# A decoder layer on one core: attention scores in 32-row tiles opened and closed in two halves, k spread by GpSimd alone, and linear attention's turns, h and statistics at other places

## The reference

```python
# block 1
x = x + linear_attention(layernorm(x, ln1))  # 16 heads of 8; phi = elu + 1
#   kv = einsum('bshd,bshe->bhde', phi_k, v); z = sum_s phi_k
#   out = (phi_q kv) / (phi_q z + 1e-6) @ wo
x = x + lookup_gelu(layernorm(x, ln2) @ w1) @ w2   # input rounded to steps of 0.1
# block 2: cross attention with ctx, causal, rows of the queries masked
q, k, v = x @ WQ, ctx @ WK, ctx @ WV               # 16 heads of 8
scores = where(mask | future, -1e9, q k / sqrt(8)); out = softmax(scores) v @ WO
# block 3: a mixture of experts
out = x @ W_shared.T + (sum of the two gate weights) * (x @ W_expert.T) + bias
```

## Time and profile before

| | us |
|---|---|
| median of 3 runs | 599.19 (598.56 to 599.45) |
| the profiled execution | 602.87 |
| its span | 601.2 |
| TensorE busy | 527.9 (88%) |
| VectorE busy | 416.3 (69%) |
| ScalarE busy | 369.0 (61%) |
| GpSimd busy | 330.8 (55%) |

### The profile page before, as it was taken

One profiled execution on the slowest core, in us unless ns is written; L12 is line 12 of the kernel. 1 busy time (PEld: TensorE's weight loads), 2 busy tenths in 40 slices (PEclk: granted clock), 3 DMA queues, 4 the chain that ended last, 5 costly groups with the idle time before them and its releaser, 6 DMA issues.

```text
span 601.2 us, 22996 instructions
## 1 busy us (share of the span) xinstructions
PE 527.9 (88%) x9312; PEld 370.4 (62%) x9312; DVE 416.3 (69%) x1453; ACT 369.0 (61%) x643; POOL 330.8 (55%) x603
## 2 busy tenths in 40 slices
PE   2699998989999999988999999998989989999741
PEld 1467776656677767755666666666646656666530
DVE  2567777766767765375587778777867787779743
ACT  2356566557777777766766666666656666666520
POOL 6766667745755556341337554655465447554563
PEclk9899999999999999999999999999999999999876
DMA  5610000000000001001112111111111011111001
GB/s 160 188 38 3 3 1 2 3 3 1 1 2 1 2 5 26 1 11 28 27 32 49 29 40 33 49 30 43 29 48 28 27 48 50 28 34 22 20 19 35
DMA packets 24986, 17.97 MB, mean 30 GB/s; under 512 B 3120, under 2 KB 21424, under 8 KB 24880
## 3 DMA queue, kind: packets, MB, share of 16 engines
q1 hardware_dynamic: 24448, 16.43, 10.4%
q10 hardware_dynamic: 432, 0.07, 0.1%
HBM read 9.67 MB, written 4.19 MB: 23 GB/s over the span
## 4 chain that ended last, share of the span: by engine, by line
PE 58%; SPq 9%; ACT 8%; DVE 7%; issue 7%; POOL 6%; DMA 4%; POOLq 0%; DVEq 0%; ACTq 0%
SPq L394 8%; PE pair L1145 7%; PE pair L1179 7%; PE pair L1194 6%; PE pair L1213 6%; PE pair L1258 5%; PE pair L1114 5%; PE pair L1223 4%; PE pair L1036 4%; DMA k_exp<-k_sb 3%; ACT gel L718 3%; PE pair L1107 3%; PE pair L1232 2%; PE pair L1201 2%; PE pair L1049 2%
## 5 line engine op out<-in xcount | busy, mean ns | idle before, releaser
L718 ACT ACTIVATE gel<-pair 128x1024 f32<-128x1024 f32 x64 | 65.5, 1024 | 75.4 <-PE pair L1213 75.4
L926 DVE TENSOR_REDUCE neg_max<-pair 128x16 f32<-128x1024 f32 x64 | 60.9, 951 | 20.3 <-PE pair L1201 20.2
L1194 PE MATMUL pair<-k_exp,qT 64*32 64x256 f32 (+1 forms) x1024 | 57.5, 501 | 8.5 <-DMA k_exp<-k_sb 7.7
L1179 PEld LDWEIGHTS pair<-w,gel 128*128 128x128 f32 x512 | 60.3, 192 | 7.4 <-issue 5.5
L1223 PEld LDWEIGHTS pair<-v,gel 128*32 128x32 f32 x4096 | 41.7, 110 | 37.1 <-ACT gel L718 31.2
L1179 PE MATMUL pair<-w,gel 128*128 128x128 f32 x512 | 62.2, 276 | 1.0 <-ACT gel L643 1.0
L1223 PE MATMUL pair<-v,gel 128*32 128x18 f32 x4096 | 48.2, 187 | 15.5 <-ACT gel L718 12.8
L1145 PE MATMUL pair<-hT,w 128*128 128x512 f32 x128 | 58.5, 597 | 1.9 <-ACT lev L638 1.3
L712 ACT ACTIVATE gel<-gel,row_scale 128x512 f32<-128x512 f32 x80 | 54.4, 719 | 4.8 <-DVE gel L939 4.8
L303 POOL TENSOR_SCALAR veps_c<-mv_c 128x4 f32<-128x4 f32 x16 | 3.7, 229 | 96.0 <-issue 89.8
L303 POOL TENSOR_SCALAR veps_b<-mv_b 128x4 f32<-128x4 f32 x32 | 7.8, 245 | 81.6 <-DVE mv_b L295 45.8
(11 more groups left out here) (127 smaller groups left out, 1228.5 us busy)
## 6 DMA issues: line engine op xcount, KB each, us to landing
X<-in_x SPq DMA_DIRECT2D x16, 256.0 KB, 3.0
cT<-in_ctx SPq DMA_DIRECT2D x16, 256.0 KB, 2.9
out_rows<-X SPq DMA_DIRECT2D x16, 256.0 KB, 2.5
k_exp<-k_sb SPq DMA_DIRECT2D x160, 16.0 KB
w<-in_L_attn_w SPq DMA_DIRECT2D x2, 256.0 KB, 3.3
w_kv<-in_L_attn_wk SPq DMA_DIRECT2D x1, 64.0 KB, 3.2
w_q<-in_L_attn_wq ACTq DMA_DIRECT2D x1, 64.0 KB, 3.0
w_kv<-in_L_attn_wv SPq DMA_DIRECT2D x1, 64.0 KB, 3.1
```

What stands on the lines that cost most here:

```text
L718: nc.scalar.activation(pT[par], pair[par][:, :, :].rearrange("p a c -> p (a c)"), ACT.Copy).then_inc(pT_ready, 1)
L926: nc.vector.tensor_reduce(neg_max[par][:, :].rearrange("p (a h) -> p a h", a=2), scores, AX.X, ALU.max, negate=True).then_inc(max_ready, 1)
L1179: last = nc.tensor.matmul(bank(6 + q)[:, P * t:P * (t + 1)], gel[:, q, f, P * t:P * (t + 1)], w_2[:, f, :], start=(f == 0), stop=(f == NF ...
L1194: nc.tensor.matmul(pair[t % 2][b * QW:(b + 1) * QW, half, 0:HH * width], qT[p][rows, batch + first:batch + first + QW], keys, start=True, ...
```

## The change

- `k_exp` has 4 copies (HQ) instead of 8: in copy h only head h of each 32 rows is not zero. GpSimd makes all four with `quad_mask`; the DMAs, `kexp_loaded`, `zeroed` and the memsets are gone.
- A tile's scores are 16 matmuls on 32 rows each, of half the columns. `scores_open(n)` does the mask first, then quads 0 and 2; `scores_close(n)` waits for the opening (`s_opened`) and does quads 1 and 3. The two quads of a half write different columns of the same bank. Tile n + 2 is opened ahead of `weigh_values(n)`; tile n + 1 is closed at the head of slot t.
- Phase 1: TensorE turns the rows of s + 2 ahead of the k and v projection; ScalarE makes h ahead of the exponentials of k and the copy of v; VectorE attends ahead of phi_q and takes the statistics one group earlier, at the stage's end.
- GpSimd's constants go in five parts behind its stages 3 to 7 of phase 2, VectorE's behind stage 11. The first probabilities and the rows of ln_a change places on ScalarE.

```diff
@@ SyncE, phase3
-                if exists(s + 1):
-                    spread_k(s + 1, 1 - p)
@@ GpSimd
+            def late_constants(part):
+                if part == 0:
+                    const(nc.gpsimd.memset(quad_mask[:, :], 1.0))
+                    for b in range(4):
+                        m = quad_mask[b * QW:(b + 1) * QW, :]
+                        const(select(out=m, in_=m, compare_op=ALU.is_ge, fill=0.0, base=0,
+                                     pattern=[[-DH, HQ]], channel_multiplier=1))
...
+                if part == 1:
+                    const(nc.gpsimd.memset(causal[:, :, :], 0.0))
...
-                for h in range(HDMA, HH):
+                for h in range(HQ):
                     last = nc.gpsimd.tensor_scalar(k_exp[q][:, h, :], k_sb[:, :],
-                                                   half_mask[:, h:h + 1], 0.0, ALU.mult, ALU.add)
+                                                   quad_mask[:, h:h + 1], 0.0, ALU.mult, ALU.add)
...
-            for s in range(2):
-                zero(k_exp[s])
-
-            pipeline(pool, phase2, first=2, last=NG - 4)
+
+            for s in range(2, NG - 3):
+                phase2(s, s % 2)
+                if 3 <= s <= 7:
+                    pool.wait_ge(ln_a.offs, 2 * s)
+                    late_constants(s - 3)
@@ ScalarE, phase1: rows_h and rows_h2 ahead of the exponential of k and the copy of v
@@ ScalarE, head of phase 3
+            probabilities(0)
             rows_a(NG - 3, 1)
-            probabilities(0)
+            act.wait_ge(down_done, NG)
+            phase3(0, 0, slots=(0, 1))
             rows_a(NG - 2, 0)
-            act.wait_ge(down_done, NG)
-            phase3(0, 0, slots=(0,))
+            phase3(0, 0, slots=(2,))
             rows_a(NG - 1, 1)
-            phase3(0, 0, slots=range(1, TG))
+            phase3(0, 0, slots=(3,))
@@ VectorE, phase1
-                if exists(s + 3):
-                    statistics1(s + 3, 1 - p)
-                if second_norm(s + 3):
-                    statistics2(s + 3 - NG, 1 - p)
+                if s < 0:
+                    statistics1(2, 0)
+                if exists(s):
+                    attend(s, p)
...
-                if exists(s):
-                    attend(s, p)
...
+                if exists(s + 4):
+                    statistics1(s + 4, p)
+                if second_norm(s + 4):
+                    statistics2(s + 4 - NG, p)
@@ TensorE, phase1: xpose_rows and xpose_rows2(0) ahead of the k and v projection
@@ TensorE, phase2, stage NG - 1
-                    first_scores(0, 0)
+                    scores_open(0)
                 for t in range(TG):
+                    if t == 1 and s == NG - 1:
+                        scores_close(0)
@@ TensorE, phase3
+            def quad_scores(n, quads):
+                t, p = n % TG, n // TG % 2
                 first, width = (0, QW) if n % 2 else (QW, S)
+                for quad in quads:
+                    rows = slice(quad * QW, (quad + 1) * QW)
+                    heads = slice(quad % 2 * HQ * width, (quad % 2 + 1) * HQ * width)
                     for b in range(QB):
                         batch = (t // 2 * QB + b) * S
+                        last = nc.tensor.matmul(
+                            pair[t % 2][b * QW:(b + 1) * QW, quad // 2, heads],
+                            qT[p][rows, batch + first:batch + first + QW],
+                            k_exp[p][rows, :, batch:batch + width],
+                            start=False, stop=quad % 2 == 1)
+                return last
+
+            def scores_open(n):
+
+                after(pe, pT_ready, n - 1)
+                if n % TG == 0:
+                    pe.wait_ge(kexp_ready, n // TG + 1)
+                    pe.wait_ge(q_ready, n // TG + 1)
+                width = QW if n % 2 else S
                 for half in range(2):
                     rows = slice(half * FH, half * FH + QW)
                     future = causal_bf[rows, :].rearrange("p (h k) -> p h k", k=S)[:, :, S - width:]
                     for b in range(QB):
+                        nc.tensor.matmul(pair[n % 2][b * QW:(b + 1) * QW, half, 0:HH * width],
+                                         ident_bf[rows, rows], future, start=True, stop=False)
+                quad_scores(n, (0, 2)).then_inc(s_opened, 1)
+
+            def scores_close(n):
+
+                pe.wait_ge(s_opened, n + 1)
+                quad_scores(n, (1, 3)).then_inc(s_done, 1)
...
                 for t in slots:
-                    if t < TG - 1 and exists(s):
-                        scores(s * TG + t + 1, t + 1, p)
+                    if s == 0 and t == 0:
+                        scores_open(1)
+                    elif exists(s) and s * TG + t + 1 < NT:
+                        scores_close(s * TG + t + 1)
...
-                    if t == TG - 1 and exists(g):
-                        first_scores(g, q)
...
+                        if s * TG + t + 2 < NT:
+                            scores_open(s * TG + t + 2)
                         weigh_values(s * TG + t, t, p)
```

More of the change, by code:

```diff
@@ L153, in decoder_layer @@
             arena = early_memory.enter_context(nc.sbuf_tensor("arena", [P, ARENA], F32))
-        k_exp = [sb(f"k_exp{i}", [P, HH, GW]) for i in range(2)]
+        k_exp = [sb(f"k_exp{i}", [P, HQ, GW]) for i in range(2)]
         used = 0
@@ L223, in decoder_layer @@
             ("s_done", "max_ready", "sub_ready", "exp_ready"))
+        s_opened = sem("s_opened")
         p_xposed, pT_ready, pv_done = sem("p_xposed"), sem("pT_ready"), sem("pv_done")
@@ L454, in _ @@
                 rows1(i, i)
[L455 to L473, removed]
             def phase1(s, p):
@@ L615, in phase1 @@
                                          scale=-1.0).then_inc(expq_ready, 1)
+                if exists(s + 2):
+                    rows_h(s + 2, p)
+                if second_norm(s + 2):
+                    if s + 2 == NG:
+                        act.wait_ge(w_loaded, ALL_WEIGHTS)
+                    rows_h2(s + 2 - NG, p)
+                if exists(g):
                     act.wait_ge(kv_done, g + 1)
@@ L1018, in _ @@
             pipeline(dve, phase1, last=NG - 1)
-            pipeline(dve, phase2, first=0, last=NG // 2 - 1)
+            pipeline(dve, phase2, first=0, last=NG - 5)
             constants()
-            pipeline(dve, phase2, first=NG // 2, last=NG - 1)
+            pipeline(dve, phase2, first=NG - 4, last=NG - 1)
             phase3(-1, 1, slots=(2, 3))
@@ L1110, in phase1 @@
                     numerators(s, p)
+                if exists(s + 2):
+                    xpose_rows(s + 2, p)
+                if s + 2 == NG:
+                    xpose_rows2(0, p)
                 if exists(g):
@@ L1183, in phase2 @@
                     last.then_inc(down_done, 1)
-            def scores(n, t, p):
-                after(pe, pT_ready, n - 1)
+            def quad_scores(n, quads):
+                t, p = n % TG, n // TG % 2
                 first, width = (0, QW) if n % 2 else (QW, S)
-                for half in range(2):
-                    rows = slice(half * FH, (half + 1) * FH)
+                for quad in quads:
+                    rows = slice(quad * QW, (quad + 1) * QW)
+                    heads = slice(quad % 2 * HQ * width, (quad % 2 + 1) * HQ * width)
                     for b in range(QB):
                         batch = (t // 2 * QB + b) * S
-                        keys = k_exp[p][rows, :, batch:batch + width]
-                        nc.tensor.matmul(pair[t % 2][b * QW:(b + 1) * QW, half, 0:HH * width],
-                                         qT[p][rows, batch + first:batch + first + QW], keys,
-                                         start=True, stop=False)
+                        last = nc.tensor.matmul(
[10 more added lines that the diff above has]
+                width = QW if n % 2 else S
                 for half in range(2):
@@ L1200, in scores @@
                     for b in range(QB):
-                        last = nc.tensor.matmul(pair[t % 2][b * QW:(b + 1) * QW, half, 0:HH * width],
-                                                ident_bf[rows, rows], future,
-                                                start=False, stop=True)
-                last.then_inc(s_done, 1)
+                        nc.tensor.matmul(pair[n % 2][b * QW:(b + 1) * QW, half, 0:HH * width],
[4 more added lines that the diff above has]
+                quad_scores(n, (1, 3)).then_inc(s_done, 1)
             def turn_probabilities(n, t):
@@ L1274, in phase3 @@
                         turn_y(g)
+                    if s == 0 and t == 0:
+                        scores_close(1)
                     if exists(s):
```

44 lines of the change are left out of this document (18 added, 26 removed).

## The result

The changed kernel takes **593.42 us** (median of 6 runs, 592.41 to 594.35), against 598.16 for the kernel before beside it (6 runs, 595.4 to 599.45): ratio 0.9926, interval 0.9907 to 0.9945. It was measured again later, beside 13 runs of the kernel before: 592.85 against 600.15, ratio 0.9898 [0.985, 0.9945]. The forecast was 593.1.

The account below looks back on a forecast made before the run. TensorE was taken as the bound, so other engines' steps pay only where it waits. -10.7 + 3.2 + 5.6 - 3.6 - 0.6 = -6.1 us, from the median 599.19 to 593.1 us; range 585 to 602.5, the forecast's own 590 to 597.

Parts of the forecast that it names:

- Part 1: Cross attention: GpSimd alone spreads k in four copies, so TensorE's DMA waits go; minus 10.7 us.
- part 2: Cross-attention scores in two halves: one more instruction group a tile, fixed cost partly shared with the mask; plus 3.2 us.
- rival (e): Cross attention: DMAs go but the wait stays, now for GpSimd's four copies; 604 us, chance 0.01.
- (b): Scores: each group keeps its own fixed part, 7.0 us more, 600.1 us; chance 0.13.
- (c): Scores: the small tiles' weight loads aren't covered, 0.21 us a tile, 606 us; chance 0.1.
- Part 3: Linear attention: statistics behind phi_k hold kv_sum and transposes join the loop; period 7.3 against 6.86, plus 5.6 us.
- Rival (a): Linear attention: the statistics don't hold the loop, part 3 costs nothing, 587.5 us; chance 0.17.
- Rival (d): Linear attention: TensorE idles 1.3 of 7.3 us and falls to its lower clock, 600 us; chance 0.1.
- Part 4: Start: GpSimd's constants move away from ahead of group 2's rows, ending TensorE's wait and slow start; minus 3.6 us.
- Part 5: Feed-forward: k_exp memsets go, ending TensorE's wait for ScalarE's h; returning constants stay hidden; minus 0.6 us.

Follow-up runs that it names:

- stats_back: The changed kernel with VectorE's linear-attention statistics put back between kv_sum and attend: 588.46 us, ratio 0.9834 to the kernel before.
- early_consts: The changed kernel with GpSimd's five constants made in one go near the start, ahead of group 2's rows: 597.03 us, ratio 0.9944 to the kernel before.
- old_phase1: The changed kernel with phase 1 of TensorE, ScalarE and VectorE in the order of the kernel before: 590.0 us, ratio 0.9821 to the kernel before.
- before_again: The kernel before, unchanged, run once more for a second profile: 598.96 us in one execution, span 597.2.
- pool8: The kernel before with all eight 64-row copies of k made by GpSimd, no DMAs or k_exp memsets: 606.6 us, ratio 1.0101.
- pool8_nobias: pool8 with GpSimd's bias add on the mixture's output replaced by a one-input multiplication by one: 590.39 us, ratio 0.9834 to the kernel before.
- pool8_nocopy: pool8 with VectorE's copy of top_z replaced by a maximum of the same tile with itself: 605.87 us, ratio 1.0122 to the kernel before.
- one_piece: The changed kernel with each tile's scores opened right ahead of their closing, not one slot earlier: 606.89 us, ratio 1.0105 to the kernel before.

## Why the prediction was right

The forecast was 593.1, the result 593.42. This is better than its steps were. Beside its own runs of the kernel before, the changed kernel gained 4.7 us (598.16 to 593.42), and 7.3 the second time, where 6.1 was forecast. By its own parts:

**Part 1** (-10.7) and **part 2** (+3.2) together said -7.5. Measured between the two profiled executions: -9.2 in 13 periods and -0.8 in the last stage, -10.0. Part 1's step held: a stage without a DMA wait took 19.05, an undisturbed stage of the changed kernel takes 19.02, and ScalarE's copy is next late, as said. But the mean stage is 19.17, so 1.9 us of the gain over 13 stages is missing: the stage without a wait was taken as the mean one. GpSimd's four copies take 2.69, and no opening waits for them (rival (e) is out).

**Part 2** was mis-sized. The added group should have cost 0.16, of which 0.12 were to be shared with the mask. Measured, the mask gives up its 0.12 (0.34 to 0.22) and the two halves take 0.55 + 0.59 = 1.14 against 1.02, so that the fixed part of the added group is 0.12: together 0.00, below both bounds. That refutes (b), two full fixed parts, and (c), bare weight loads, 0.21 a tile; the time that the page cited under (c) would have given did not come. The rule of the Trainium skill (TensorEngine Tiling (Array Packing), Key Properties) agrees in so far as mask and first half, now in one tiling mode, lie closer; that a drain is what the 0.12 were is not shown.

**Part 3** (+5.6) had the mechanism, and stats_back shows it by itself. Its size was wrong: the 13 periods are 92.20 us against 89.23, +3.0 instead of +5.6; a plain period is 7.07, not 7.3. From the k, v projection (51.82) phi_k ends at 3.80, not 4.0; kv_sum starts at 5.13, not 5.3; its hand-over to the numerators is 0.05, not 0.15. phi_k's earlier end is also what brings kv_sum forward. Two terms of the loop, priced 0.2 and 0.1 too long, count 13 times each. Rival (a) said that the statistics wouldn't hold the loop; they do. Rival (d): the clock is 1.00 from 27 to 126, so with the short waits there (0.34 and 0.27) it did not come down.

**Part 4** (-3.6): the third group's kv products start at 34.48 instead of 36.55, -2.1; in the second profiles at 32.17 instead of 35.51, -3.3. early_consts and old_phase1 show that the constants are the cause. Most of the size is the clock (0.50 from 25 to 30 us before), which the changed kernel's first profile also had at 0.68 from 20 to 25; the forecast took the slow start as gone.

**Part 5** (-0.6): from the last kv products (0.9 later than before) to the feed-forward's start at 159.53 (159.60 before) the gain is 1.0, and by 249 us it is 1.4. There is no wait near 160. The five pieces of constants are hidden, as forecast.

Sum of these as measured: +0.9 up to the last kv products, -1.4, -9.2, -0.8: **-10.5**, not -6.1. Taken from the median of 599.19, as I did it, this would have been 588.7. What made the forecast right is a second error of the same size: I carried the 3.7 us by which the profiled execution lay above the median over to the new kernel. But this excess was for the most part in what the change takes away. Another execution of the kernel before (before_again) was 3.9 us shorter, 1.0 of that at the start and 2.1 in the 13 periods with the DMA waits, while the changed kernel's profiled execution lies at the low end of its own runs, 1.0 below their median. The gain should have been counted from a typical execution: from 256.26, part 1 is 8.6 instead of 10.7. Two errors of some 4.5 us cancelled, and that was luck.

## What to carry to other kernels

A wait for DMAs varies from execution to execution: size it from more than one execution, or count a stage without it as the floor and its mean as uncertain. Before two profiles are compared, read the granted clock stretch by stretch: here it made one and the same kernel's start differ by 2.3 us (34.48 and 32.17). Work moved on an engine that has slack on average can still lengthen a loop if it lands between two steps of the chain that closes it; place it where that engine waits anyway. Before a GpSimd queue is made longer, look at which small VectorE instructions will fall beside it.

## What the hardware showed that was not expected

**VectorE is held while GpSimd works, for some instructions only.** A copy of 128x4 numbers took 170 ns in the kernel before and 1476 ns in the mean in pool8, up to 2.05 us, ending with GpSimd's bias add; a TENSOR_TENSOR in its place 1361. In the changed kernel VectorE's bn_stats (380.73, 0.88 us for four) run at full speed beside the same bias add (380.55 to 381.83), in VectorE's timeline:

```profile
380.73 0.88 DVE L286 BATCH_NORM_STATS2 stats_b<-X 128x6 f32<-128x128 f32 x4 [0.17 <-DVE X L985]
```

The Trainium skill, SBUF — State Buffer, "SBUF: two separate sides", says that VectorE and GpSimd share one pair of ports as an exclusive lock, which VectorE needs for an instruction in a 2-port mode or with two SBUF inputs. These rows agree: the copy and the TENSOR_TENSOR of SBUF tiles are held, bn_stats with one input is not. By the page the loser waits for one whole instruction. In pool8_nobias that is so: no copy of top_z waits beyond the end of the GpSimd instruction that runs when it comes. In pool8 and pool8_nocopy it isn't. Where the instruction came during the eighth copy of k, nine times in each, it waited for the bias add behind it as well (1.68 to 1.92 us). Where it came during the seventh, six times, it got in five times at that one's end, though the eighth follows without a gap; the sixth is the row at 382.88. One of the five, with the next VectorE instruction, which is held in its turn:

```profile
422.96 2.04 POOL L502 TENSOR_SCALAR k_exp<-k_sb,half_mask 128x512 f32<-128x512 f32 x3
...
424.06 0.29 DVE L945 COPY top_z<-top 128x4 f32<-128x4 f32 x1
424.38 1.89 DVE L947 TENSOR_TENSOR top<-top,top_z 128x32 f32<-128x32 f32 x1
...
424.95 1.28 POOL L529 TENSOR_TENSOR moe_out<-moe_out,bias_bc 128x512 f32<-128x512 f32 x1
```

So VectorE doesn't need a gap in GpSimd's queue. Why it never got in ahead of the bias add stays open.

**A signal of TensorE to itself costs 0.15 us** when nothing lies between, as one_piece shows, 7.8 us in 52 tiles; from start to start the first half then takes 0.21 us longer.
